# Graph attention kernel: three step buffers, more compares on VectorE, sums and reciprocals on GpSimd

## The chip, the cores and the metric

The kernel runs on one core of a Trainium2 chip. The metric is the device time of one execution in microseconds, lower is better. PE is TensorE's matmul (PEld its weight load), DVE is VectorE, ACT is ScalarE, POOL is GpSimd, and SP is the engine whose queue issues most DMAs.

## The reference

One graph attention layer with a residual and a layer norm. B = 8 batches, N = 2048 nodes, F = 512 features, H = 8 heads of O = 64.

```
h   = x @ W[head]                                  (per batch and head)
s1  = h . a1[head];  s2 = h . a2[head]
e   = leaky_relu(s1[i] + s2[j], slope 0.2)
att = softmax over j of (e where adj[i, j] > 0, else a very negative number)
out = layernorm(x + concat over heads of att @ h)
```

## The kernel before

The softmax is never formed. exp(leaky_relu(s1 + s2)) is a product of a factor of i and a factor of j on either side of the sign of s1 + s2. So the kernel needs only 0/1 masks (adjacency and sign) as stationary operands of matmuls: one set, m_pos, where the sum is positive, and one, m_neg, where it isn't. The denominators are a 65th column of the same matmuls.

A **unit** is one head of one block of 512 nodes i. There are 4 blocks and 32 units in a batch, 256 units in all; k counts blocks, h heads, u all units. Work on the engines for a unit:

- PE `spread_s1` (L449) spreads the head's row of s1 over 128 partitions of a PSUM bank. It is done two units ahead, between the halves of a unit.
- ACT `compare` (L607) makes the step of s1 + s2 for most of the 16 chunks of j (128 nodes each), 512 wide, into m_pos. DVE `compare` (L811) makes the others from s1_bc, a copy that SP loads from DRAM (`load_s1`, L311). `dve_slots` says which chunks are DVE's.
- DVE `make_pos` (L825, twice) ands the step with the transposed adjacency maskT; `make_neg` (L832) makes m_neg from both.
- PE multiplies: the positive half, 64 matmuls of 130 columns (L530) into banks 0 and 1; then the negative half, 128 of 65 columns (L561, L562) into bank 2 or 3.
- DVE `take_pos` (L670) empties banks 0 and 1 (semaphore pos_read, which PE wants before the next positive half). DVE `take_neg` scales the negative half (L677), adds both (L679) and inverts the denominators (L681). POOL `divide_unit` scales these (L991) and multiplies (L996) into y.

m_pos, m_neg, total and s1_bc have two buffers each. A compare for a unit therefore waits until the unit two before it has been multiplied and its m_neg made. DVE's order in the iteration of unit u is: masks of u + 1 with take_pos(u) between m_pos and m_neg, a maximum over a tile of x, statistics or normalisation if any, compare(u + 2), take_neg(u). For the last unit of a batch all the masks of the next batch's unit 0 come before take_pos.

Ahead of the units of a batch stands the **projection**: 16 chunks, for which PE multiplies x by W in float32 (L499, eight matmuls a chunk, three banks in turn) and DVE writes high parts and products (`split_chunk`: L794, L796, L797, L799), POOL the low parts (L1035, L1037). Within it DVE also makes the step and masks of unit 1 (and 0 in the first batch). Its next batch's x tiles are loaded, transposed (L416) and copied (L579) in units 0 to 22 of the batch before; the score matmuls (L427, L435, L456, L462) are in units 24 to 27, and the statistics in units 28 to 30: `score_maxima`, an all-reduce on POOL (`spread_maxima`, L982), `exponents`, `no_edge` and `turn_s2` (L767 last), which the next compare of unit 0 waits for.

The adjacency for the next block comes in eight pieces: SP loads, ACT cuts to 8 bits (L573), SP transposes (L323). In the first block of a batch all eight are cut in unit 0's iteration on ACT, that is during the projection; in the others one or so per unit.

A finished block gets its residual x by an accumulating DMA from POOL (`residual`, L1002) in head 0 of the next block; `ln_first_half`, `ln_statistics` and `ln_apply` (L686, L690, L703) stand in heads 1, 2 and 3, POOL's `deviation` (a pow, L986) in head 3, and the store in SP's queue at head 5.

Of the kernel before, what the change touches and what calls it, by code (L numbers as in the profile page):

```python
# [20 lines left out]
P = 128  # L21
# [22 lines left out]
DVE_SLOTS = {1: {0: (7,), 1: ()}, 2: {0: (7,), 1: (7,)}, 3: {0: (6, 7), 1: (7,)}}  # L44
# [17 lines left out]
def gat_kernel(nc, x, adj, W, a1, a2, out):  # L62
# [39 lines left out]
    with ExitStack() as ctx:  # L102
# [34 lines left out]
        m_pos = [sb(f"m_pos{i}", [P, JC // 2, 2 * BLK], FP8) for i in range(2)]  # L137
# [37 lines left out]
        prod_d = sb("prod_d", [P, 512], F32)  # L175
        x_sum = sb("x_sum", [P, F], F32)

        mean_f = sb("mean_f", [P, H, O1], F32)
        mean_part = sb("mean_part", [P, H, O1], F16)
# [4 lines left out]
        den_inv = [sb(f"den_inv{i}", [P, IT], F32) for i in range(2)]  # L184
# [68 lines left out]
        neg_made = sem("neg_made", free=1)  # L253
# [3 lines left out]
        pos_summed = sem("pos_summed", free=1)  # L257
# [49 lines left out]
        def _(sp):  # L307
# [53 lines left out]
            for q in range(PIECES):  # L361
                if q == 4:
                    store_s1(0)
                    sp.wait_ge(s1_stored, 16 * KB)
                    load_s1(0, 0)
                    load_s1(1, 1)
# [4 lines left out]
            with nc.Fori(0, B, engines=[sp.engine], hint_back_edge=True) as b:  # L371
                for k in range(KB):
                    g = b * KB + k
                    for h in range(H):
# [5 lines left out]
                        if unit == UNITS - 2:  # L380
                            sp.wait_ge(s1_stored, 16 * KB * (b + 2))
                        load_s1(u + 2, h % 2)
# [10 lines left out]
                        for t in range(JC):  # L393
                            if LOAD_UNIT[t] == unit > 0:
                                load_x(JC * (b + 1) + t, t % 2, ((b + 1) * (JC // 2) + t // 2) % (NBLK * IT // 2))
                        if unit == STURN_UNIT + 1:
                            store_s1(b + 1)
                        if h == 5:
# [12 lines left out]
        def _(pe):  # L411
# [35 lines left out]
            def spread_s1(unit):  # L447
# [37 lines left out]
            for unit in range(2):  # L485
                spread_s1(unit)

            with nc.Fori(0, B, engines=[pe.engine], hint_back_edge=True) as b:
                for jc in range(JC):
                    if jc == 0:  # L490
                        pe.wait_ge(s1_T_copied, b + 1)
                    if jc == 1:
# [9 lines left out]
                for k in range(KB):  # L502
                    g = b * KB + k
                    for h in range(H):
# [11 lines left out]
                        for qd in range(QUADS):  # L516
# [5 lines left out]
                            for it in range(IT):  # L522
                                acc = slot(0, it)
                                for j in range(qd * JQ, (qd + 1) * JQ):
# [3 lines left out]
                                    mask = chunk(m_pos[hp], j, it * P, P).bitcast(FP8_WIDE)  # L528
# [8 lines left out]

                        if unit == UNITS - 2:
                            pe.wait_ge(s1_T_copied, b + 2)
                        spread_s1((unit + 2) % UNITS)  # L540
# [16 lines left out]
                        for it in range(IT):  # L557
                            acc = ps[:, 2 + hp, it * O1:(it + 1) * O1]
# [528 lines left out]
```

## Time and profile before

| what | value |
| --- | --- |
| median of 3 runs | 2871.23 us (2862.51 to 2875.33) |
| profiled execution, own time | 2872.58 us |
| its span | 2870.6 us |
| PE / DVE / ACT / POOL busy | 2669.8 / 2510.0 / 2337.4 / 1077.6 us |
| mean granted clock of PE | 0.978 |
| chain that ended last, by engine | ACT 36%, PE 28%, DVE 16%, issue 13%, DMA 3% |

Busy times are unions over a span in which stages differ, so a high share doesn't name the bound; the stages are read one by one further down. The chain follows the last instruction back through what released each step. A wait for several semaphores is shown under the one that came last.

### The profile page before, as it was taken

Reading aid. Unit: us, or ns where it says so; the run is one execution under the profiler, and the core shown is the slowest. Engines: PE = TensorE matmul, PEld = TensorE weight load, DVE = VectorE, ACT = ScalarE, POOL = GpSimd, SP = SyncE. Lnnn points to the kernel's source line nnn. Section 1 sums busy time; section 2 is a strip of 40 time slices with the busy share of each in tenths; the row PEclk is TensorE's granted clock in tenths of the full one; section 3 lists DMA queues with packets and bytes.
Section 4 is the critical chain, followed back from the end, with each engine's and each line's share of the span. In section 5 each row is a group of like instructions: output and inputs, shape, how many; then the busy total and the mean of one; then the engine's idle time right before and its main releaser. Section 6 shows DMA issues by size and latency. Waiting matters only on the chain.

```text
span 2870.6 us, 126143 instructions
## 1 busy us (share of the span) xinstructions
PE 2669.8 (93%) x52546; PEld 2317.7 (81%) x52546; DVE 2510.0 (87%) x3828; ACT 2337.4 (81%) x3894; POOL 1077.6 (38%) x1011
## 2 busy tenths in 40 slices
PE   6999999999999899999999999899998999899996
PEld 3699867988589895898949998499984998759986
DVE  6898978999789988899888998889988999889996
ACT  3699974999669994799938998399983999839995
POOL 4633335333343324433253332633326233263332
PEclk9999999999999999999999999999999999999998
DMA  6467652676527754377543775447744577445773
GB/s 177 119 132 175 150 141 72 142 173 143 142 65 165 175 137 117 72 177 169 136 104 87 176 164 128 118 93 174 165 120 120 111 173 150 124 105 126 175 150 99
DMA packets 281206, 390.20 MB, mean 136 GB/s; under 512 B 161857, under 2 KB 161857, under 8 KB 280673
## 3 DMA queue, kind: packets, MB, share of 16 engines
q1 hardware_dynamic: 253536, 315.24, 41.4%
q0 software_dynamic: 27136, 67.12, 15.0%
q8 instruction: 424, 6.95, 1.0%
q14 instruction: 110, 0.89, 0.1%
HBM read 313.52 MB, written 34.14 MB: 121 GB/s over the span
## 4 chain that ended last, share of the span: by engine, by line
ACT 36%; PE 28%; DVE 16%; issue 13%; DMA 3%; POOL 1%; DVEq 0%; ACTq 0%; SPq 0%; POOLq 0%
ACT m_pos L607 33%; PE ps L530 10%; PE ps L499 5%; PE ps L561 5%; PE ps L562 5%; DMA y<-in_x 3%; DVE m_neg L832 3%; ACT adj_cut L573 2%; DVE m_pos L825 2%; DVE prod L796 2%; ACT xT L579 1%; DVE prod_d L799 1%; DVE m_pos L811 1%; DVE b_both L794 1%; PE ps L435 1%
## 5 line engine op out<-in xcount | busy, mean ns | idle before, releaser
L607 ACT ACTIVATE m_pos<-ps,s_steep 128x512 fp8e4<-128x512 f32 x3440 | 2092.7, 1068 | 354.0 <-PE ps L449 302.8
L530 PE MATMUL ps<-b_both,m_pos 128*128 128x130 f16 x16384 | 1019.4, 221 | 80.3 <-DVE total L670 52.0
L561 PE MATMUL ps<-d_hi,m_neg 128*128 128x65 f16 x16384 | 1039.1, 194 | 20.6 <-issue 20.2
L562 PE MATMUL ps<-d_lo,m_neg 128*128 128x65 f16 x16384 | 1038.7, 194 | 7.1 <-issue 6.7
L562 PEld LDWEIGHTS ps<-d_lo,m_neg 128*128 128x128 fp8e5 x16384 | 1010.3, 98 | 38.8 <-issue 25.4
L530 PEld LDWEIGHTS ps<-b_both,m_pos 128*128 128x128 fp8e5 x16384 | 964.2, 98 | 92.5 <-issue 91.4
L561 PEld LDWEIGHTS ps<-d_hi,m_neg 128*128 128x128 fp8e5 x16384 | 1019.7, 98 | 17.6 <-issue 17.2
L825 DVE TENSOR_TENSOR m_pos<-m_pos,maskT 128x1024 uint32<-128x1024 uint32 x512 | 633.0, 1255 | 156.1 <-ACT m_pos L607 140.0
L991 POOL TENSOR_TENSOR den_scaled<-den_inv,bound 128x4 f32<-128x4 f32 x256 | 251.3, 982 | 1260.5 <-DVE den_inv L681 1204.0
L832 DVE TENSOR_TENSOR m_neg<-m_pos,maskT 128x2048 uint32<-128x2048 uint32 x256 | 583.8, 2280 | 0.3
L499 PE MATMUL ps<-W_sb,xT 128*128 128x512 f32 x1024 | 461.7, 612 | 45.3 <-DVE prod_d L799 43.4
L573 ACT ACTIVATE adj_cut<-adj_in 128x1024 fp8e4<-128x1024 int32 x264 | 367.5, 1456 | 118.1 <-DMA adj_in<-in_adj 118.1
L499 PEld LDWEIGHTS ps<-W_sb,xT 128*128 128x128 f32 x1024 | 199.7, 197 | 301.9 <-issue 241.7
L811 DVE TENSOR_SCALAR m_pos<-s_bc,s_neg 128x512 fp8e5<-128x512 f32 x656 | 282.3, 482 | 10.4 <-DVE s_neg L767 4.3
L996 POOL TENSOR_TENSOR y<-total,den_scaled 128x256 f32<-128x256 f32 x256 | 281.0, 1098 | 22.6 <-POOL den_scaled L991 2.3
L533 PE MATMUL ps<-mean,tiny_bf 128*128 128x65 f16 x1024 | 198.9, 194 | 0.0
L670 DVE TENSOR_REDUCE total<-ps 128x260 f32<-128x520 f32 x256 | 176.7, 690 | 22.4 <-PE ps L530 21.9
L1035 POOL TENSOR_TENSOR b_both<-prod,b_both 128x512 f16<-128x512 f32 x128 | 143.8, 1124 | 101.2 <-DVE prod L796 90.3
L1037 POOL TENSOR_TENSOR d_lo<-prod_d,d_hi 128x512 f16<-128x512 f32 x128 | 177.4, 1386 | 8.9
L579 ACT ACTIVATE xT<-ps 128x512 f32<-128x512 f32 x144 | 149.2, 1038 | 22.9 <-PE ps L416 22.9
L969 POOL DMA_DIRECT2D x_sum<-in_x x128 | 118.3, 924 | 105.0 <-DMA x_sum<-in_x 97.5
L677 DVE TENSOR_TENSOR neg_part<-ps,r_row 128x260 f32<-128x260 f32 x256 | 107.0, 418 | 30.1 <-PE ps L562 29.6
(94 smaller groups left out, 1552.3 us busy)
## 6 DMA issues: line engine op xcount, KB each, us to landing
adj_in<-in_adj SPq DMA_DIRECT2D x266, 512.0 KB, 4.8
s_bc<-s_rows SPq DMA_DIRECT2D x258, 256.0 KB, 3.6
x_in<-in_x SPq DMA_DIRECT2D x134, 256.0 KB, 4.1
x_sum<-in_x POOLq DMA_DIRECT2D x128, 256.0 KB, 4.8
y<-in_x POOLq DMA_DIRECT2D x32, 1024.0 KB, 11.0
out<-y SPq DMA_DIRECT2D x32, 1024.0 KB, 7.4
maskT<-adj_cut SPq DMA_TRANSPOSE x264, 3.9
m_neg<-in_x SPq DMA_DIRECT2D x10, 256.0 KB, 3.7
```

What stands on the lines that cost most here:

```text
L499: mm = pe.matmul(ps[:, H_BANKS[jc % 3], :], xT[:, fc, jc * P:(jc + 1) * P], W_sb[:, fc, :], start=(fc == 0), stop=(fc == FC - 1))
L530: mm = pe.matmul(acc, mask, b_both[:, j, h, :, :], start=(j == 0 and it % 2 == 0), stop=(j == JC - 1 and it % 2 == 1))
L533: pe.matmul(acc[:, 0:O1], tiny_bf[:], mean[:, h, :], start=False, stop=False)
L561: pe.matmul(acc, mask, d_hi[:, j, h, :], start=(j == 0), stop=False)
L562: mm = pe.matmul(acc, mask, d_lo[:, j, h, :], start=False, stop=(j == JC - 1))
L573: nc.scalar.activation(adj_cut8[slot][:], adj_in[slot][:], ACT.Relu, scale=STEEP, saturate=False).then_inc(adj_cut, 1)
L607: ins = nc.scalar.activation(chunk(m_pos[h % 2], j, 0, BLK), ps[:, BANK_S1 + h % 2, :], ACT.Relu, bias=s2_steep[:, j, h:h + 1], scale=STEE ...
L811: ins = V.tensor_scalar(chunk(m_pos[hp], j, 0, BLK).bitcast(FP8_WIDE), s1_bc[hp][:], s2_neg[:, j, h:h + 1], STEP_UP, ALU.is_gt, ALU.mult, ...
L825: V.tensor_tensor(words(m_pos[hp][:, js, :]), words(m_pos[hp][:, js, :]), words(mask[:, js, :]), ALU.bitwise_and).then_inc(pos_made, 1)
L832: V.tensor_tensor(words(m_neg[hp][:]), words(m_pos[hp][:]), words(mask[:]), ALU.bitwise_xor).then_inc(neg_made, 1)
L991: G.tensor_tensor(den_scaled[hp][:], den_inv[hp][:], bound[:].to_broadcast([P, IT]), ALU.mult).then_inc(den_made, 1)
L996: G.tensor_tensor(y[par][:, :, h * O:(h + 1) * O], total[hp][:, :, 0:O], den_scaled[hp][:].unsqueeze(2).to_broadcast([P, IT, O]), ALU.mult ...
```

## The change

- m_pos gets a third buffer, indexed by unit % 3. Compares may run up to two units ahead on ACT; DVE compares unit u + 3 in the iteration of u, and `before(unit)` counts how many units back the buffer's last user is, across the batch's end (32 is no multiple of 3). Unit 2 of each batch is compared during the projection.
- `DVE_SLOTS` and `dve_slots` give DVE 115 chunks a batch by the new rules (82 by the old).
- DVE's order in the iteration of u becomes: make_neg(u + 1), the maximum, take_pos(u), statistics or normalisation, make_pos(u + 2), compare(u + 3), then the scaling of the negative half.
- `take_neg` keeps only the scaling, into one of two buffers neg_part; POOL does the add and inverts with a pow to the power of -1 in `divide_unit`. mean_part now lies in prod_d's memory.
- `spread_s1` runs three units ahead, in the middle of the negative half, and waits for ACT's compare of the unit that used the bank. `load_s1` is three units ahead too.
- The normalisation, deviation and store of a block stand one unit later; `copy_s1` stands in the last unit.

```diff
-DVE_SLOTS = {1: {0: (7,), 1: ()}, 2: {0: (7,), 1: (7,)}, 3: {0: (6, 7), 1: (7,)}}
+DVE_SLOTS = {1: {0: (7,), 1: (7,)}, 2: {0: (6, 7), 1: (7,)}, 3: {0: (6, 7), 1: (6, 7)}}
@@ dve_slots
-        k, h = divmod((unit - 2) % UNITS, H)
-        if unit in (0, 1) or k * H + h == STAT_UNIT:
+        k, h = divmod((unit - 3) % UNITS, H)
+        if unit in (0, 1, 2) or k * H + h == STAT_UNIT:
             return DVE_SLOTS[1]
-        if (k and h in (2, 3)) or k * H + h in (0, STAT_UNIT + 1):
+        if k and h in (3, 4):
             return DVE_SLOTS[2]
         return DVE_SLOTS[3]
+    def before(unit):
+        return {0: UNITS - (UNITS - 2), 1: UNITS + 1 - (UNITS - 1), 2: UNITS + 2 - (UNITS - 3)}.get(unit, 3)
@@ buffers
-        m_pos = [... for i in range(2)]
+        m_pos = [... for i in range(3)]
-        neg_part = sb("neg_part", [P, IT, O1], F32)
+        neg_part = [sb(f"neg_part{i}", [P, IT, O1], F32) for i in range(2)]
@@ SP, the first batch's unit 2, behind the pieces of unit 0
+                        if unit == 0:
+                            with sp.If(b < 1):
+                                load_s1(2, 0)
+                            load_s1(u + 3, (h + 1) % 2)
@@ PE
+            def spread_s1(unit, u):
+                if type(u) is not int:
+                    pe.wait_ge(step_act, at(step_act, QUADS * (u - 1)))
...
+                    if jc == 8:
+                        spread_s1(2, b * UNITS + 2)
...
-                        spread_s1((unit + 2) % UNITS)
...
                         for it in range(IT):
+                            if it == IT // 2 and unit < UNITS - 3:
+                                spread_s1(unit + 3, u + 3)
@@ DVE take_neg
-                V.tensor_tensor(total[hp][:], total[hp][:], neg_part[:], ALU.add).then_inc(total_made, 1)
-                dve.wait_ge(total_made, u + 1)
-                V.reciprocal(den_inv[hp][:], total[hp][:, :, O]).then_inc(den_inverted, 1)
@@ DVE, iteration of a unit
-                        if unit == UNITS - 1:
-                            with dve.If(b < B - 1):
-                                make_masks(u + 1, 0, maskT[0], g + 1)
-                            take_pos(u, h)
...
+                        if unit < UNITS - 1:
+                            make_neg(u + 1, unit + 1)
...
+                        take_pos(u, h)
...
-                        for when, work in ((1, ln_first_half), (2, ln_statistics), (3, ln_apply)):
+                        for when, work in ((2, ln_first_half), (3, ln_statistics), (4, ln_apply)):
...
+                        if unit < UNITS - 2:
+                            for qd in range(QUADS):
+                                make_pos(u + 2, unit + 2, qd, g + 1)
+                        if unit < UNITS - 3:
+                            compare(u + 3, unit + 3, g * (H // 2) + (h + 3) // 2)
@@ POOL divide_unit
+                G.tensor_tensor(total[hp][:], total[hp][:], neg_part[hp][:], ALU.add).then_inc(total_made, 1)
+                pool.wait_ge(total_made, u + 1)
+                G.tensor_tensor(den[hp][:], total[hp][:, :, O], minus_one[:], ALU.pow).then_inc(den_inverted, 1)
                 pool.wait_ge(den_inverted, u + 1)
-                G.tensor_tensor(den_scaled[hp][:], den_inv[hp][:], bound[:].to_broadcast([P, IT]), ALU.mult
+                G.tensor_tensor(den_scaled[hp][:], den[hp][:], bound[:].to_broadcast([P, IT]), ALU.mult
```

## Rows read from the trace of the kernel before

**Rows 1.** The page: busy time, share of the span, instructions, by engine.
```profile
PE 2669.8 (93%) x52546; PEld 2317.7 (81%) x52546; DVE 2510.0 (87%) x3828; ACT 2337.4 (81%) x3894; POOL 1077.6 (38%) x1011
```

**Rows 2.** Windows: stretch, length, busy us of each engine (instructions), granted clock, DMA share.
```profile
1445.12:1508.72 63.60, 57.57 (x129) 25.13 (x129) 53.60 (x90) 22.24 (x33) 40.37 (x35) 0.95 0.44 113
...
1165.50:1232.52 67.02, 67.02 (x1602) 66.08 (x1600) 58.54 (x82) 63.57 (x109) 19.07 (x21) 0.97 0.42 85
...
1232.52:1303.66 71.14, 67.44 (x1612) 65.67 (x1610) 66.74 (x96) 71.14 (x122) 24.16 (x23) 1.00 0.75 175
...
1375.51:1445.12 69.61, 68.76 (x1578) 62.87 (x1576) 60.10 (x100) 61.08 (x105) 18.60 (x20) 1.00 0.51 126
```

**Rows 3.** Timeline of PE: start, length, engine, line, operation, xcount, [idle before it].
```profile
1184.29 0.38 PE L449 MATMUL ps<-s_T,s_pick 96*128 96x512 bf16 x1
...
1192.10 0.38 PE L449 MATMUL ps<-s_T,s_pick 96*128 96x512 bf16 x1
...
1200.39 0.38 PE L449 MATMUL ps<-s_T,s_pick 96*128 96x512 bf16 x1
...
1450.80 4.88 PE L499 MATMUL ps<-W_sb,xT 128*128 128x512 f32 x11
...
1461.71 4.63 PE L499 MATMUL ps<-W_sb,xT 128*128 128x512 f32 x5 [6.03 <-DVE prod_d L799]
...
1513.45 1.00 PE L530 MATMUL ps<-b_both,m_pos 128*128 128x130 f16 x13 [2.23 <-POOL b_both L1035]
```

**Rows 4.** Timeline of ACT, around unit 2's compare in two batches, and one unit.
```profile
1167.08 8.20 ACT L607 ACTIVATE m_pos<-ps,s_steep 128x512 fp8e4<-128x512 f32 x14 [36.74 <-PE ps L449]
...
1217.19 7.62 ACT L607 ACTIVATE m_pos<-ps,s_steep 128x512 fp8e4<-128x512 f32 x13 [0.25 <-PE ps L449]
...
1516.48 8.20 ACT L607 ACTIVATE m_pos<-ps,s_steep 128x512 fp8e4<-128x512 f32 x14 [36.42 <-PE ps L449]
```

**Rows 5.** Timeline of DVE: the end of one unit, and the batch's end.
```profile
1213.34 1.27 DVE L811 TENSOR_SCALAR m_pos<-s_bc,s_neg 128x512 fp8e5<-128x512 f32 x3
...
1214.52 0.42 DVE L677 TENSOR_TENSOR neg_part<-ps,r_row 128x260 f32<-128x260 f32 x1
...
1215.62 2.58 DVE L825 TENSOR_TENSOR m_pos<-m_pos,maskT 128x1024 uint32<-128x1024 uint32 x2
...
1441.25 0.22 DVE L767 TENSOR_SCALAR s_neg<-s_col 128x128 f32<-128x128 f32 x1
...
1458.97 0.90 DVE L794 TENSOR_TENSOR b_both<-ps,k_b 128x512 f16<-128x512 f32 x1
```

**Rows 6.** POOL's L991 and L986 (ns min/median/max), then timelines of POOL and DVE.
```profile
L991 POOL TENSOR_TENSOR den_scaled<-den_inv,bound x256: 191/1209/1269, 122.8 to 2849.6; 128x4 f32<-128x4 f32 x128
...
L986 POOL TENSOR_TENSOR ln_rstd<-ln_var,minus_half x32: 1036/1037/1063, 208.7 to 2863.2; 128x4 f32<-128x4 f32 x32
...
1259.47 1.04 POOL L986 TENSOR_TENSOR ln_rstd<-ln_var,minus_half 128x4 f32<-128x4 f32 x1 [4.93 <-DVE ln_var L698]
...
1259.54 0.89 DVE L811 TENSOR_SCALAR m_pos<-s_bc,s_neg 128x512 fp8e5<-128x512 f32 x2
...
1279.59 0.61 POOL L996 TENSOR_TENSOR y<-total,den_scaled 128x256 f32<-128x256 f32 x1
...
1279.62 1.66 DVE L825 TENSOR_TENSOR m_pos<-m_pos,maskT 128x1024 uint32<-128x1024 uint32 x1 [0.17 <-ACT m_pos L607]
```

**Rows 7.** One wait of the whole span; timelines of DVE, POOL, SP's queue.
```profile
DVE ln_stats L686 <- DMA y<-in_x: 42.2, 13, 10.3
...
1419.88 0.16 DVE L722 TENSOR_REDUCE stat<-xmax 128x1 f32<-128x16 f32 x1
...
1433.98 0.19 POOL L991 TENSOR_TENSOR den_scaled<-den_inv,bound 128x4 f32<-128x4 f32 x1 [6.94 <-issue]
...
97.45 2.28 DVE L832 TENSOR_TENSOR m_neg<-m_pos,maskT 128x2048 uint32<-128x2048 uint32 x1
...
108.17 11.66 SPq L311 DMA_DIRECT2D s_bc<-s_rows  x2
```

More of the change, by code:

```diff
@@ L364, in _ @@
                     sp.wait_ge(s1_stored, 16 * KB)
-                    load_s1(0, 0)
-                    load_s1(1, 1)
+                    for unit in range(2):
+                        load_s1(unit, unit)
                 turn_piece(q, q % 2, 0, q // 2)
@@ L379, in _ @@
                                 store_block(g - 1, 1)
-                        if unit == UNITS - 2:
+                        if unit == UNITS - 3:
                             sp.wait_ge(s1_stored, 16 * KB * (b + 2))
-                        load_s1(u + 2, h % 2)
+                        if unit == UNITS - 1:
+                            sp.sem_inc(waited[sp.engine], 1)
+                            with sp.If(b < B - 1):
+                                load_s1(u + 3, (h + 1) % 2)
+                        elif unit:
+                            load_s1(u + 3, (h + 1) % 2)
                         for t in range(JC):
@@ L527, in _ @@
                                         pe.sem_inc(waited[pe.engine], 1)
-                                    mask = chunk(m_pos[hp], j, it * P, P).bitcast(FP8_WIDE)
+                                    mask = chunk(m_pos[unit % 3], j, it * P, P).bitcast(FP8_WIDE)
                                     mm = pe.matmul(acc, mask, b_both[:, j, h, :, :], start=(j == 0 and it % 2 == 0),
@@ L606, in compare @@
                             j = qd * JQ + c
-                            ins = nc.scalar.activation(chunk(m_pos[h % 2], j, 0, BLK), ps[:, BANK_S1 + h % 2, :], ACT.Relu,
+                            ins = nc.scalar.activation(chunk(m_pos[unit % 3], j, 0, BLK), ps[:, BANK_S1 + unit % 2, :], ACT.Relu,
                                                        bias=s2_steep[:, j, h:h + 1], scale=STEEP, saturate=False)
@@ L799, in split_chunk, with compare @@
                 V.tensor_tensor(full_d, bank, kd, ALU.mult).then_inc(hi_d_made, 1)
-            def compare(u, h, nth, unit):
+            def compare(u, unit, nth):
+                h = unit % H
                 hp = h % 2
-                dve.wait_ge(neg_made, at(neg_made, u - 1))
+                dve.wait_ge(neg_made, at(neg_made, u - before(unit) + 1))
                 dve.sem_inc(waited[dve.engine], 1)
@@ L824, in make_pos, with make_neg @@
                 js = slice(qd * JQ // 2, (qd + 1) * JQ // 2)
[L825 removed]
+                V.tensor_tensor(words(m_pos[unit % 3][:, js, :]), words(m_pos[unit % 3][:, js, :]),
                                 words(mask[:, js, :]), ALU.bitwise_and).then_inc(pos_made, 1)
[L828 to L829 removed]
+            def make_neg(u, unit):
+                mask = maskT[unit // H % 2]
                 dve.wait_ge(unit_done, at(unit_done, u - 1))
                 dve.wait_ge(pos_made, at(pos_made, QUADS * (u + 1)))
[L832 removed]
+                V.tensor_tensor(words(m_neg[unit % 2][:]), words(m_pos[unit % 3][:]), words(mask[:]), ALU.bitwise_xor
                                 ).then_inc(neg_made, 1)
[L835 to L841 removed]
             V.nop().then_inc(x_maxed, start[x_maxed])
```

102 lines of the change are left out of this document (51 added, 51 removed).

## The prediction

> **What bounds the kernel now.** The page first: all of TensorE, VectorE and ScalarE look loaded, 93, 87 and 81% [rows 1], so no average decides and the stages must be read. The windows show one batch's stages: the projection (63.6 us, the 16 chunks of L499) and three of the four blocks of eight units [rows 2]. In block 1 ScalarE is busy 71.14 of 71.14 us: it sets the pace, and block 2 is built alike. In block 0, where it has no adjacency pieces to cut, TensorE is busy all 67.0 us, and block 3 is nearly so (68.8 of 69.6). In the projection ScalarE stands idle 36 us, until the first compare of unit 2 [rows 4], although it is the engine that is short later: m_pos has two buffers, and unit 2's is unit 0's.
>
> TensorE's own need comes from its timeline [rows 3]: from one spread of s1 to the next a unit takes 1192.10 - 1184.29 = 7.81 us, with a transposed tile of x 1200.39 - 1192.10 = 8.29. Blocks: 0: 8 x 7.81 + 6 x 0.48 = 65.4; 1 and 2: 62.5 + 5 x 0.48 = 64.9 each; 3, with no transposes but the score and mean matmuls, about 71 (its window's 68.8 busy, and unit 24 starts some 3 us ahead of it). Sum 266. A batch lasts 1516.48 - 1167.08 = 349.4 us [rows 4], less the projection's 63.6: the unit phase takes 285.8. So 20 us of it are waits, half-clock stretches and unit 0's late start. The projection has its own: TensorE idles 6.03 us after three chunks, for VectorE's prod_d, and the next five matmuls take 4.63 us, where eleven took 4.88 just before the stall [rows 3]: it comes back at 1.2 GHz. Undisturbed, 128 matmuls at the 0.43 us of the eleven are 55 us; 8.7 could go.
>
> **The parts.** *Compares.* By the new slots VectorE has 115 compares a batch, by the old 82 (656 over 8 batches). One costs VectorE 0.40 us (three from 1213.34 to 1214.52 [rows 5]) and saves ScalarE 0.58 (thirteen in 7.62 [rows 4]). Per full block 8 move: ScalarE 71.1 - 4.6 = 66.5, VectorE + 3.2.
>
> *Add and reciprocal.* L677 to the next L825 is 1215.62 - 1214.52 = 1.10 us [rows 5]; 0.42 stays and about 0.03 between instructions: VectorE loses 0.65 a unit, 5.2 a block. Block 1: 66.7 - 5.2 + 3.2, and 0.4 of gaps, is 65.1 us, against TensorE's 64.9. Block 2 is taken the same. All three engines then need 65 to 67 us in blocks 1 and 2: balanced, with little to spare.
>
> *GpSimd.* Each unit gains an add (nearest row: the 128x256 multiply L996, 0.61 us) and a pow (L986, same size and operation, 1.04 us whenever it ran) ahead of the 0.20 and 0.61 that it has [rows 6]: 2.5 us of 8, and its idle time covers that; total has two buffers, so it may end two units later. What can't be read off is what this takes from VectorE. L996 began at 1279.59, just ahead of L825 at 1279.62, and that L825 took 1.66, where two back to back take 2.58 [rows 5]; the other way round L991's median is 1.21 us against a least of 0.19, since it starts with an L825 and waits behind it [rows 6]. So the two exclude each other. The pow seems harmless: it ran 1259.47 to 1260.5 and the two compares that started under it took 0.89, as two always do. Bounds a unit: nothing, and 0.61 + 1.04 + 0.20 + 0.61 = 2.46 if each op blocks for its whole length. The add starts when the 2.28 us m_neg starts and so waits behind it, then runs under the maximum or take_pos, which no row shows blocked; the last multiply now falls on L825 or the compares, where before it mostly met take_pos. I take 0.35 more a unit, one hit of 0.4 in most units, 2.8 a block: VectorE needs 67.9 in blocks 1 and 2.
>
> The Trainium skill ("SBUF — State Buffer", Who interferes with whom) says that a VectorE instruction with two SBUF inputs and a GpSimd one that reads SBUF exclude each other for the whole instruction, whichever issues first going first. The 1.66 agrees; the pow over the compares doesn't show a hold of its whole length. By the rule alone the sum would go to the 2.46.
>
> *Three buffers, order.* ScalarE may compare unit 2 in the projection and be up to two units ahead; it saves a unit's 8 us at the start of each batch. A unit's masks are made one and a half units before TensorE wants them, so a late VectorE stops TensorE only through take_pos, whose bank is wanted again 3.9 us later (the negative half). That cover holds one lag of 3 to 3.5 us. The normalisation puts 5.2 us into three units running, so it is exceeded in blocks 1 and 2, and the 3.0 us by which each of these blocks overruns comes on top: I take 5 us of TensorE's waits a batch. The spread of s1 moves into the negative half at the same 0.22 us, and now waits for ScalarE's compare of two units before, long done.
>
> *Normalisation later.* It waits 42.2 us in 13 places for the residual's DMA [rows 7]; issued about 5 us into a block, and landing some 11 us later (the last block's wait is 10.3), it is in before the third unit reads it, but the last block's 10.3 stays. This is inside the 20 us above, not added. Stores and deviation move with it, no queue behind them is short.
>
> *Batch's end.* The negative half of unit 30, neg(30), starts a unit and a half, 11.8 us, before TensorE's projection at 1445.12. Now s2_neg is made at 1441.25, 8 us into it; ScalarE's compare of the next unit 0 waits for that, unit 0's masks wait for the compare, and take_pos(31) stands behind the masks. VectorE reaches its first chunk 13.85 us after TensorE's, at 1458.97 [rows 5]. In the new order the scores are turned 3 to 6 us into neg(30) and compare(0) ends 11 to 14 us into it: VectorE's first chunk comes 5 to 9 us after TensorE's, and TensorE, three banks ahead, is released at about its 10.3. The stall and its 1.2 GHz stretch go: 8.7 us a batch, in seven batches. Unit 0 waits 2.23 us for the last b_lo [rows 3]; I leave 1.5.
>
> *New waits.* GpSimd's next arithmetic after stat_made (1420.04) is at 1433.98; the all-reduce is between [rows 7]; with an add and a pow queued behind that, take_pos(30) comes 2 to 3 us late: 3 us a batch. In batch 0 alone, load_s1(2) stands in SP's queue behind the pieces of unit 0, at 108 us; VectorE is then at its tenth chunk at 97.5 [rows 7], and waits about 11 with the landing. At the end, add and pow on GpSimd for 0.65 on VectorE: 1.7.
>
> **Sum**, against the profiled execution's 2872.58 (span 2870.6; the median is 2871.23, so the same to 0.1%). Unit phase: 266 + 5 + 3 + 1.5 = 275.5, say 276: 285.8 - 276 = 9.8, times 8, 78. Projection: 7 x 8.7 = 61. Batch 0: -11. Tail: -1.7. 2872.6 - 126 = 2746; I say 2745, 4.4% faster. This case alone: 2700 to 2790 (VectorE's 0.35 between 0.1 and 0.7).
>
> **Rivals.** *TensorE alone sets the pace.* Blocking costs nothing: 266 + 3 a batch, 135 + 61 - 13 = 183 off, 2690. For: VectorE's 65.1 is level with 64.9. Against: the L825 of 1.66.
> *GpSimd's lock eats half.* Each unit loses 0.8 us (the multiply's whole 0.61 and the scaling's 0.20): VectorE needs 65.1 + 6.4 = 71.5 in blocks 1 and 2 and 66 and 71 in the others, unit phase 281 to 283, 2790 to 2810.
> *Slower.* One mechanism: pow and add hold the port to their end and the chain falls on two-input work each time. VectorE's average unit, about 8.0 (65.1 / 8 in block 1, less in block 0), must then grow past the present 285.8 / 32 = 8.93 and the 0.27 a unit that the projection gives back: from 1.2 us a unit. At the full 2.46, less about 0.6 that lies under take_pos and maxima, it is 9.9 a unit, 317 a batch, 8 x 31 - 48 = 200 slower: 3070. For: the 1.66 us; against: the compares under L986 at full speed. The Trainium skill's rule above is on this rival's side.
> *No change.* ScalarE stays the bound in spite of its 8 fewer compares, since it cannot start until the spread in the middle of the negative half; then blocks 1 and 2 stay at 70 and only the projection's gain is left: 2820 to 2860.
>
> **Chances.** My forecast 0.57, TensorE alone 0.12, half eaten 0.15, little or no change 0.08, slower 0.08. Range 2685 to 2835: from the first rival to the start of the last ones. Faster by over 0.5% 0.86, within 0.5% 0.06, slower 0.08; 0.5% is what a measurement of this kernel tells from nothing.
>
> **What would show it.** Right: TensorE's 6 us wait in the projection gone and the stage near 55; ScalarE's 36 us wait cut by a compare of 8; blocks 1 and 2 at 66 to 68 us; some L825 or L811 at 1.5 times their length under GpSimd's multiply; one wait near 11 us at VectorE in batch 0. Wrong: long L825, L832 or L811 under the pow; take_pos waiting for GpSimd's multiply all through; ScalarE busy all of blocks 1 and 2.

## The result, and the profile after

The change makes the kernel 0.6% faster: 2848.94 us (median of 8 runs) against 2864.81 us for the kernel before, run beside it; the ratio is 0.9943, 95% interval 0.9925 to 0.996. The forecast was 2745 us. The profiled execution has a span of 2845.0 us.

The page's busy line and the chain of work that ended last:

```profile
PE 2666.2 (94%) x52546; PEld 2314.2 (81%) x52546; DVE 2501.7 (88%) x3580; ACT 2190.7 (77%) x3630; POOL 1919.3 (67%) x1524
...
PE 53%; DVE 20%; issue 12%; ACT 6%; POOL 4%; DMA 3%; SPq 1%; DVEq 1%; ACTq 0%; POOLq 0%
```

ScalarE lost 147 us of work [rows 1] and fell from 36% of the chain to 6%. The load moved as planned, yet the time hardly did. The windows of one batch: its projection, blocks 0 to 3 and the pause behind it (columns as in [rows 2], engines PE, PEld, DVE, ACT, POOL):

```profile
1099.50:1154.75 55.25, 55.25 (x129) 24.42 (x130) 51.00 (x87) 23.03 (x35) 41.09 (x37) 1.00 0.51 124
1154.75:1226.31 71.56, 68.57 (x1601) 67.08 (x1600) 65.63 (x82) 53.70 (x91) 51.87 (x37) 0.95 0.39 92
1226.31:1294.77 68.46, 65.58 (x1603) 64.19 (x1599) 64.91 (x87) 66.81 (x111) 50.03 (x37) 1.00 0.75 177
1294.77:1365.12 70.35, 66.24 (x1602) 64.48 (x1599) 65.14 (x89) 67.31 (x112) 51.91 (x40) 1.00 0.74 171
1365.12:1441.80 76.68, 73.65 (x1637) 67.59 (x1633) 60.01 (x97) 57.51 (x98) 42.58 (x39) 0.98 0.50 126
1441.80:1444.54 2.74, 0.06 (x3) 0.01 (x1) 1.23 (x1) 2.74 (x5) 0.00 (x0) 1.00 0.02 6
```

The projection is at 55.25 us, where it was 63.60 [rows 2]. In blocks 1 and 2 ScalarE is no longer busy throughout, but neither is another engine: 66.8 and 67.3 us for ScalarE, 65.6 and 66.2 for TensorE, 64.9 and 65.1 for VectorE, in stages of 68.5 and 70.4. Block 3 is longer than before, and the last window is new.

The waits that answer to those of before (engine, line, what it waited for: us in total, times, longest):

```profile
ACT xT L603 <- PE ps L431: 234.2, 20, 27.8
DVE m_pos L850 <- ACT m_pos L632: 118.8, 83, 2.8
PE ps L551 <- DVE total L694: 28.3, 26, 3.1
PE ps L520 <- issue: 20.3, 7, 3.4
PE ps L551 <- issue: 18.2, 18, 2.6
PE ps L585 <- issue: 15.1, 23, 2.5
DVE ln_stats L707 <- DMA y<-in_x: 14.6, 4, 12.3
PE ps L586 <- issue: 7.3, 10, 1.3
```

ScalarE's idle time of 36 us in the projection [rows 4] is still 27 us long, now ahead of the first tile copy: it has done unit 2's compare and has nothing more it may do. The residual's wait fell from 42.2 us [rows 7] to 14.6.

### The profile page after: what moved, and what is told of

Its sections match the earlier page's. It is cut to its first block, busy times and chain, and to the rows that moved or that the text cites. A ratio compares the mean times of both kernels' runs of the same rounds, so it can differ in the third digit from the quotient of the medians.

```text
span 2845.0 us, 127095 instructions
## 1 busy us (share of the span) xinstructions
PE 2666.2 (94%) x52546; PEld 2314.2 (81%) x52546; DVE 2501.7 (88%) x3580; ACT 2190.7 (77%) x3630; POOL 1919.3 (67%) x1524
## 3 DMA queue, kind: packets, MB, share of 16 engines
q8 instruction: 432, 7.08, 1.1%
## 4 chain that ended last, share of the span: by engine, by line
PE 53%; DVE 20%; issue 12%; ACT 6%; POOL 4%; DMA 3%; SPq 1%; DVEq 1%; ACTq 0%; POOLq 0%
PE ps L551 20%; PE ps L585 10%; PE ps L586 10%; PE ps L520 7%; ACT m_pos L632 5%; DVE m_pos L850 4%; DVE m_pos L836 3%; DVE m_neg L857 3%; DMA adj_in<-in_adj 2%; DVE prod L819 1%; DVE total L694 1%; PE ps L450 1%; PE ps L431 1%; DVE prod_d L822 1%; DVE y L724 1%
## 5 line engine op out<-in xcount | busy, mean ns | idle before, releaser
L632 ACT ACTIVATE m_pos<-ps,s_steep 128x512 fp8e4<-128x512 f32 x3176 | 1906.2, 902 | 178.6 <-PE ps L468 90.6
L585 PE MATMUL ps<-d_hi,m_neg 128*128 128x65 f16 x16384 | 1076.3, 194 | 15.1 <-issue 15.1
L586 PE MATMUL ps<-d_lo,m_neg 128*128 128x65 f16 x16384 | 1075.0, 194 | 7.6 <-issue 7.3
L585 PEld LDWEIGHTS ps<-d_hi,m_neg 128*128 128x128 fp8e5 x16384 | 1039.1, 98 | 18.6 <-issue 17.6
L1014 POOL TENSOR_TENSOR total<-total,neg_part 128x260 f32<-128x260 f32 x256 | 600.9, 2347 | 513.9 <-DVE neg_part L702 447.9
L850 DVE TENSOR_TENSOR m_pos<-m_pos,maskT 128x1024 uint32<-128x1024 uint32 x512 | 619.0, 1237 | 120.2 <-ACT m_pos L632 118.8
L597 ACT ACTIVATE adj_cut<-adj_in 128x1024 fp8e4<-128x1024 int32 x264 | 315.5, 1258 | 189.9 <-DMA adj_in<-in_adj 189.8
L836 DVE TENSOR_SCALAR m_pos<-s_bc,s_neg 128x512 fp8e5<-128x512 f32 x920 | 446.2, 544 | 10.9 <-DMA s_bc<-s_rows 6.6
L1016 POOL TENSOR_TENSOR den<-total,minus_one 128x4 f32<-128x4 f32 x256 | 313.5, 1225 | 20.2
L603 ACT ACTIVATE xT<-ps 128x512 f32<-128x512 f32 x144 | 113.9, 791 | 234.3 <-PE ps L431 234.2
L1018 POOL TENSOR_TENSOR den_scaled<-den,bound 128x4 f32<-128x4 f32 x256 | 164.5, 643 | 20.1
```

The costliest lines, as they stand in the source:

```text
L585: pe.matmul(acc, mask, d_hi[:, j, h, :], start=(j == 0), stop=False)
L586: mm = pe.matmul(acc, mask, d_lo[:, j, h, :], start=False, stop=(j == JC - 1))
L597: nc.scalar.activation(adj_cut8[slot][:], adj_in[slot][:], ACT.Relu, scale=STEEP, saturate=False).then_inc(adj_cut, 1)
L632: ins = nc.scalar.activation(chunk(m_pos[unit % 3], j, 0, BLK), ps[:, BANK_S1 + unit % 2, :], ACT.Relu, bias=s2_steep[:, j, h:h + 1], scal ...
L836: ins = V.tensor_scalar(chunk(m_pos[unit % 3], j, 0, BLK).bitcast(FP8_WIDE), s1_bc[hp][:], s2_neg[:, j, h:h + 1], STEP_UP, ALU.is_gt, ALU. ...
L850: V.tensor_tensor(words(m_pos[unit % 3][:, js, :]), words(m_pos[unit % 3][:, js, :]), words(mask[:, js, :]), ALU.bitwise_and).then_inc(pos ...
```

## TensorE's time, taken apart

For each run the start-to-start times of neighbouring matmuls in the trace were compared with the median for the same pair of lines; an excess over 0.15 us counts as a pause, under the releaser that the trace gives it. A pause "by itself" has none ("issue"): no engine and no data transfer that the profile shows was waited for. Seven steps of 0.40 us in the score matmuls (L435 before, L450 after) are the same in every batch of every run; they are work, and aren't counted as pauses. Us per batch, means of the eight; unit phase is from unit 0's first matmul to unit 31's last; VectorE's column is pauses ahead of a positive half; unit 0's holds b_lo, d_lo and slow matmuls.

| run | unit phase | by itself, in a unit | VectorE | by itself, between units | unit 0 | projection, batches 1 to 7 | at the jump |
| --- | --- | --- | --- | --- | --- | --- | --- |
| before | 286.0 | 5.8 | 7.3 | 0.8 | 3.7 | 63.7 | 0.2 |
| after | 285.7 | 5.5 | 5.3 | 1.1 | 5.3 | 56.2 | 2.7 |
| x2_old_slots | 290.7 | 6.0 | 9.3 | 1.7 | 5.0 | 56.4 | 2.6 |
| x3_norm_as_before | 293.1 | 5.0 | 12.2 | 0.3 | 5.6 | 57.3 | 2.9 |
| x5_light_vector | 284.4 | 6.2 | 1.6 | 3.1 | 5.1 | 56.9 | 2.8 |
| x6_small_pieces | 278.3 | 1.7 | 3.1 | 0.8 | 5.1 | 56.5 | 2.7 |
| x8_three_totals | 282.8 | 5.8 | 3.1 | 0.4 | 5.6 | 56.2 | 2.5 |
| x13_all_light | 276.3 | 2.5 | 0 | 1.4 | 5.1 | 57.3 | 2.5 |
| x14_before_small_pieces | 284.5 | 0.7 | 10.5 | 0.8 | 3.8 | 63.1 | 0.2 |

Without the four columns of pauses 268.5 us are left before and after, and 267 to 270 in every row; that still holds the half-speed matmuls outside unit 0, whose excess is too short to count. So the prediction's 266 us of pure work was nearly right. What failed is what it took the pauses to be. Two of them, in block 1 of the changed kernel (timeline of PE, pause in brackets):

```profile
1247.03 0.91 PE L551 MATMUL ps<-b_both,m_pos 128*128 128x130 f16 x13 [1.32 <-issue]
1252.88 0.19 PE L585 MATMUL ps<-d_hi,m_neg 128*128 128x65 f16 x1 [1.10 <-issue]
```

They come at the same few places of the program, batch after batch, most of them multiples of 123 to 126 matmuls apart. That points to the blocks in which TensorE's program is loaded. These have a DMA queue of their own; its page row, with packets, MB and share of 16 engines, is `q8 instruction: 432, 7.08, 1.1%`, so 16 KB a packet, one every 5.3 us. The packets' times in the trace bear this out. Of the 67 pauses by itself in the changed kernel (of its unit matmuls, all eight batches), 55 ended 1.25 to 1.75 us after such a packet had landed; of 38 pauses for another engine, 5 did. Before the change it was 52 of 77, and none of 50. The two pauses above end 1.45 and 1.37 us after their packet. So most of these pauses end when a block of the program has come. Why the block comes late isn't shown by this; x6 and x14 below show that the data traffic has a part in it.

## The experiments

All stand against the kernel before, run beside them.

**x1: the sum back on VectorE.** The add and the reciprocal return to `take_neg`, and the add and the pow go from `divide_unit` (not shown here).

```diff
                 V.tensor_tensor(neg_part[hp][:], neg, r, ALU.mult).then_inc(neg_read, 1)
+                V.tensor_tensor(total[hp][:], total[hp][:], neg_part[hp][:], ALU.add).then_inc(total_made, 1)
+                V.reciprocal(den[hp][:], total[hp][:, :, O]).then_inc(den_inverted, 1)
```

> The changed kernel with the add and the reciprocal back on VectorE, GpSimd as it was. Theory A (TensorE's own pace holds the time, and GpSimd's help is worth having): VectorE gets back 0.65 us a unit and loses the collisions (about 65 us in all), so 100 us more busy, of which some 40 to 60 reach the end: ratio to the kernel before about 1.01. Theory B (what GpSimd takes from VectorE's port, and the late take_pos at a batch's end behind its multiply, ate the gain): those waits go, 5 us a batch at least, ratio 0.98.

2848.29 us, 0.9929 (0.9906 to 0.9953): the same as the whole change, so neither theory was right. What moving the sums saves VectorE is worth nothing here.

**x2: the old number of compares on VectorE.** `DVE_SLOTS` as before.

```diff
-DVE_SLOTS = {1: {0: (7,), 1: (7,)}, 2: {0: (6, 7), 1: (7,)}, 3: {0: (6, 7), 1: (6, 7)}}
+DVE_SLOTS = {1: {0: (7,), 1: ()}, 2: {0: (7,), 1: (7,)}, 3: {0: (6, 7), 1: (7,)}}
```

> The changed kernel with the old table of slots: 83 compares a batch on VectorE instead of 115. Theory A (in blocks 1 and 2 TensorE and ScalarE are level, so ScalarE becomes the bound again): ScalarE needs 71 us in blocks 1 and 2 where they now take 69 and 70, so 2 to 4 us a batch more, ratio 1.00 to 1.005. Theory B (the compares are where GpSimd's multiply hits VectorE, and VectorE is the bound): ratio 0.985.

2878.8 us, 1.0034 (1.0019 to 1.005), 0.9% slower than with the 115 compares. ScalarE is late again, VectorE waits for it 261.5 us at L850 (118.8 after), and passes that on to TensorE (9.3 a batch).

**x3: the normalisation as before**, in heads 1, 2, 3, with deviation and store.

```diff
-for when, work in ((2, ln_first_half), (3, ln_statistics), (4, ln_apply)):
+for when, work in ((1, ln_first_half), (2, ln_statistics), (3, ln_apply)):
```

> The changed kernel with the normalisation, the deviation and the store back at heads 1, 2, 3 and 5. Theory A (VectorE's waits for the residual's DMA were cover that TensorE didn't notice): same as the changed kernel within 5 us, ratio 0.995. Theory B (they were on the path): 27 us of waits come back and more, since GpSimd issues the residual later, ratio 1.005.

2900.87 us, 1.0108 (1.0088 to 1.0127): the shift is worth 1.65%, the largest part of all. The unit phase is 7.4 us a batch longer, and 6.9 of that are TensorE's waits for VectorE. **x12** asks why: x1 and x3 together.

> The changed kernel with two parts undone together: the sum and the reciprocal back on VectorE (alone 0.9929) and the normalisation at its old units (alone 1.0108). Theory 1 (the shift was needed because GpSimd, with two more operations in each unit and the residual behind them, delivers a block's rows later, and VectorE waits for them): with the sums off GpSimd the rows are in time again, so a ratio of 0.993 to 0.998, and the 17 us of unit 18 go back to about 11. Theory 2 (the normalisation's place relative to VectorE's compares and ands, which now stand later in a unit, is what costs): the loss stays, 1.005 to 1.012.

2883.34 us, 1.0076 (1.005 to 1.0103). Most of the loss stays without the sums on GpSimd, so they aren't its cause. VectorE's timeline in x12, block 2, from unit 17:

```profile
1319.85 2.29 DVE L861 TENSOR_TENSOR m_neg<-m_pos,maskT 128x2048 uint32<-128x2048 uint32 x1
1322.06 0.69 DVE L694 TENSOR_REDUCE total<-ps 128x260 f32<-128x520 f32 x1
1330.21 1.29 DVE L711 BATCH_NORM_STATS2 ln_stats<-y 128x6 f32<-128x512 f32 x2 [7.46 <-DMA y<-in_x]
1331.42 2.34 DVE L854 TENSOR_TENSOR m_pos<-m_pos,maskT 128x1024 uint32<-128x1024 uint32 x2
```

In block 2 (means of six batches, counted from the block's first matmul) the residual's rows land at 24.3 us in x12 and 24.8 in x3, and VectorE comes to them at 17.1 and 15.9. In the kernel before it came at 19.4 and they landed at 21.8; with the shift it comes at 25.2 and waits in one batch of the six, 1.2 us. So of x12's longer wait (7.2 us for 2.4) about half is that VectorE comes earlier, and half that the rows land later; GpSimd issues their DMA 12.6 us into the block there and 11.0 in the kernel before, for a reason that wasn't looked into. While VectorE stands there, the masks of unit 19, take_neg(17) and take_pos(18) stand behind it; unit 18 takes TensorE 17.1 us in x12 and 10.8 after. (The slot rule stays moved in both, so the lighter units 3 and 4 no longer meet the normalisation; how much of the loss is that wasn't taken apart.)

**x4: unit 2's row loaded first in batch 0**, ahead of the pieces.

```diff
+                        else:
+                            with sp.If(b < 1):
+                                load_s1(2, 0)
...
                         if unit == 0:
-                            with sp.If(b < 1):
-                                load_s1(2, 0)
                             load_s1(u + 3, (h + 1) % 2)
```

> The changed kernel with batch 0's load of unit 2's row of s1 ahead of the eight pieces in SP's queue. The projection of batch 0 takes 66.6 us now and 59.2 before. Theory A: it goes back to 59, 7 us off, ratio 0.992. Rival: the wait only moves to another place (the adjacency pieces, delayed by the load): nothing, ratio 0.994.

2839.95 us, 0.9894 (0.9874 to 0.9913). Batch 0's projection fell from 66.6 to 60.0 us. The ratio moved by 0.5%, 14 us, twice as much; the rest has no cause shown. The wait that it removes, in the changed kernel (timelines of SP's queue and of DVE):

```profile
99.87 6.64 SPq L317 DMA_DIRECT2D s_bc<-s_rows  x3
...
105.13 0.89 DVE L836 TENSOR_SCALAR m_pos<-s_bc,s_neg 128x512 fp8e5<-128x512 f32 x2 [6.62 <-DMA s_bc<-s_rows]
```

**x5: VectorE's two ands on an eighth of the data**, which leaves out seven eighths of the masking.

```diff
-                js = slice(qd * JQ // 2, (qd + 1) * JQ // 2)
+                js = slice(qd * JQ // 2, qd * JQ // 2 + 1)
```

> The changed kernel with each and of the step and the adjacency on an eighth of its data, so it leaves out seven eighths of the masking with the adjacency; VectorE has 1.9 us less work in each unit and is nowhere the bound. What TensorE then takes is its own floor. Theory A (the floor is what the traces show when its gaps inside a unit, 15 us a batch, are counted as its own): only its 5 us a batch of waits for VectorE and part of unit 0's go, ratio to the kernel before 0.975 to 0.98. Theory B (the prediction's floor: 266 us of units and 55 of projection): ratio 0.93 to 0.94.

2847.14 us, 0.9928 (0.9899 to 0.9957). With VectorE's waits nearly gone (1.6 us a batch for 5.3) TensorE is hardly faster, and the chain says so: `PE 80%; issue 7%; DVE 4%; ...`. Theory A had expected 0.975 to 0.98; the prediction's floor (theory B) missed by more: a TensorE freed of VectorE still takes 284.4 us. Pauses by themselves are 9.3 us of that, 2.7 more than in the changed kernel.

**x6: adjacency loads an eighth as long**, to thin the traffic; it leaves out 117 of 390 MB.

```diff
-                sp.dma_start(adj_in[slot][:], adj_tiles[... slot * JH * P:(slot + 1) * JH * P]
+                sp.dma_start(adj_in[slot][:, 0:n], adj_tiles[... slot * JH * P:slot * JH * P + n]
```

> The changed kernel in which every adjacency piece after the first two loads only an eighth of its columns; seven eighths of that traffic (117 of 390 MB) are left out, every instruction is still there. Theory A (TensorE's gaps inside a unit, at fixed places of its program some 120 matmuls apart, are instruction blocks that arrive late behind the big transfers of blocks 1 and 2): 5 to 8 of the 8.4 us a batch go, ratio 0.975 to 0.98. Rival (they are something of TensorE itself): ratio 0.994, gaps as they were.

2788.24 us, 0.9727 (0.9703 to 0.9751). The waits of x6, then the rows of its queues:

```profile
PE ps L551 <- issue: 12.1, 20, 1.2
...
PE ps L586 <- issue: 1.9, 3, 0.7
...
PE ps L585 <- issue: 0.8, 2, 0.6
```

```profile
q1 hardware_dynamic: 253536, 197.80, 29.2%
...
q8 instruction: 432, 7.08, 1.1%
```

The unit phase fell by 7.4 us a batch: 3.8 of it are TensorE's own pauses in a unit (5.5 to 1.7), 2.2 are waits for VectorE. The rows of the waits say the same: the three of TensorE's unit matmuls sum to 40.6 us after the change and to 14.8 here. So about two thirds of the pauses hang on the traffic.

**x7: 128 empty instructions at the head of TensorE's program.**

```diff
+            for i in range(128):
+                pe.nop()
             pe.nop().then_inc(x_turned, start[x_turned])
```

> The changed kernel with 128 empty instructions at the head of TensorE's program, where it waits for data, so that the loop lies elsewhere in the blocks in which instructions are fetched. Between a batch's last matmul and the next one's first are 2.9 us now and were 0.2 before. Theory A (the loop's first block is fetched only on the jump, or ahead of it, according to where the loop's ends lie): the gap goes, 7 x 2.7 = 19 us, ratio 0.988. Rival (it comes with the new order): no change, ratio 0.994.

2847.28 us, 0.9926 (0.9902 to 0.995), pauses and jump unchanged. The most frequent pauses even kept their places, counted in matmuls from unit 0's first (2053 and 2177, for example), though 128 more instructions stood ahead of the loop: the places go by the loop's start and not by the program's.

**x8: a third total buffer** (in prod_d's memory), so that take_pos waits for the multiply of three units back.

```diff
-                dve.wait_ge(att_made, at(att_made, u - 1))
+                dve.wait_ge(att_made, at(att_made, u + 1 - min(before(unit), 3)))
-                V.tensor_reduce(total[hp][:], slots(0), AX.X, ALU.add).then_inc(pos_read, 1)
+                V.tensor_reduce(total[unit % 3], slots(0), AX.X, ALU.add).then_inc(pos_read, 1)
```

> The changed kernel with three buffers of the sums (the third lies in prod_d's memory), so that take_pos waits for GpSimd's multiply of three units back. At each batch's end take_pos(30) waits about 4 us for GpSimd, which was busy with the all-reduce; TensorE stands 2.7 us and runs the next 4 us at 1.2 GHz. Theory A: this goes, 4 us a batch, 30 in all, ratio 0.984. Rival (unit 0's masks need the new scores and ScalarE's compare anyhow, so the wait moves on to the projection's start): ratio 0.992 to 0.996.

2824.73 us, 0.9845 (0.98 to 0.989). This is the wait that it takes away; the changed kernel's timelines of POOL, DVE and PE at the end of a batch:

```profile
1418.07 2.30 POOL L1003 PARTITION_ALL_REDUCE stat_all<-stat  x1 [6.66 <-issue]
1428.08 0.73 POOL L1014 TENSOR_TENSOR total<-total,neg_part 128x260 f32<-128x260 f32 x1 [7.71 <-issue]
1428.89 1.06 POOL L1016 TENSOR_TENSOR den<-total,minus_one 128x4 f32<-128x4 f32 x1
1430.03 0.20 POOL L1018 TENSOR_TENSOR den_scaled<-den,bound 128x4 f32<-128x4 f32 x1
1430.31 0.61 POOL L1023 TENSOR_TENSOR y<-total,den_scaled 128x256 f32<-128x256 f32 x1
...
1431.06 0.70 DVE L694 TENSOR_REDUCE total<-ps 128x260 f32<-128x520 f32 x1 [4.37 <-POOL y L1023]
...
1432.16 0.22 PE L551 MATMUL ps<-b_both,m_pos 128*128 128x130 f16 x1 [2.56 <-DVE total L694]
...
1432.24 0.62 PE L551 MATMUL ps<-b_both,m_pos 128*128 128x130 f16 x8
...
1433.42 1.05 PE L551 MATMUL ps<-b_both,m_pos 128*128 128x130 f16 x8
```

GpSimd can do nothing between 1418 and 1428, the all-reduce; take_pos(30) waits for what is queued behind it; TensorE stands 2.56 us, runs on at full speed for 0.8 us, and then eight matmuls take 1.05 us instead of 0.62: 1.2 GHz. Two windows behind the stall (the third number from the end is the granted clock):

```profile
1432.16:1432.98 0.82, 0.82 (x16) 0.82 (x17) 0.79 (x3) 0.00 (x0) 0.75 (x1) 1.00 0.00 0
1432.98:1436.39 3.41, 3.41 (x37) 3.41 (x35) 2.75 (x7) 1.34 (x3) 1.31 (x2) 0.50 0.02 5
```

Units 30 and 31 took 10.2 and 8.7 us, and 8.1 and 7.9 in x8.

**x9, x10, x11: the two gains together, and the jump.** Between the last matmul of a batch and the first of the next the changed kernel loses 2.7 us:

```profile
1441.66 0.20 PE L586 MATMUL ps<-d_lo,m_neg 128*128 128x65 f16 x1
1444.54 1.98 PE L520 MATMUL ps<-W_sb,xT 128*128 128x512 f32 x4 [2.68 <-issue]
```

x9 has x8's and x4's edits. x10 also puts the spreads for the next batch's units 0 and 1 back ahead of the negative halves of units 30 and 31. x11 is x9 with 16 empty instructions at the end of the loop.

```diff
@@ x10, ahead of the negative half
+                        if unit >= UNITS - 2:
+                            if unit == UNITS - 2:
+                                pe.wait_ge(s1_T_copied, b + 2)
+                            spread_s1(unit + 2 - UNITS, u + 2)
@@ x11, behind the negative half
+                        if unit == UNITS - 1:
+                            for i in range(16):
+                                pe.nop()
```

> The changed kernel with both of the edits that helped: a third total buffer (0.9845 of the kernel before, alone) and batch 0's step row of unit 2 loaded ahead of the adjacency pieces (0.9894 alone). Theory 1 (the two take away different waits, of which one stands in batch 0's projection and the other at unit 31 of every batch): the gains add up to about 0.9945 - 0.9845 = 1.0% and 0.3 to 0.5%, so a ratio of 0.979 to 0.982, 2807 to 2815 us. Theory 2 (the load's gain is lost again in batch 0's first units, which wait for the block's masks): no better than the third total alone, 0.984 to 0.986.

> As the run before this one in the list (third total, load first), and the two score-row spreads for the next batch's units 0 and 1 stand before the negative half of units 30 and 31, as they do in the kernel before, not in its middle. It tells where the 2.6 to 3.9 us between the last matmul of a batch and the first of the next come from (0.2 us in the kernel before). Theory 1 (the spread and its wait in the middle of the last negative half disturb what TensorE's queue has prefetched of the loop's head): the pause falls to 0.2 us in all 7 jumps, about 19 us, 0.7% off the time. Theory 2 (it comes from the program's length or layout, or from traffic on the instruction queue at that moment): the pause stays at about 3 us and the time within 0.3% of the other run's.

> As the first run of this list (third total, load first), with 16 empty instructions on TensorE at the end of the loop's body, so that the jump stands elsewhere in the program. Theory 1 (the pause of about 3 us at the jump depends on where the jump's instruction stands relative to the blocks in which the program is fetched): the pause changes, to 0.2 us or to some other value, by more than 1 us. Theory 2 (it does not): 2.6 to 4.5 us as in the other variants, the time within 0.2% of the other run's.

x9: 2824.24 us, 0.985 (0.98 to 0.99), its four runs from 2806.4 to 2835.41. The expected sum of both gains (0.979 to 0.982) didn't come: batch 0's projection is 5.8 us shorter than in x8, but TensorE's own pauses in the profiled execution are 2.8 us a batch longer. x10: 2806.93 us, 0.9802 (0.9779 to 0.9824), four runs within 2 us. x11: 2817.89 us, 0.9828 (0.9783 to 0.9874). The pause at the jump is 2.5 to 2.7 us in all three: neither the spreads' place nor the jump's position explains it. The trace says what the pause is. The records of the loop's own branch on TensorE's sequencer (ns, least, median, most; the least is the loop's end, where it isn't taken), before and after:

```profile
L488 PEldq COMPARE_BRANCH  x8: 88/392/460, 394.2 to 2847.8; - x8
L507 PEldq COMPARE_BRANCH  x8: 88/3072/3719, 403.2 to 2821.0; - x8
```

So TensorE isn't waiting for an engine; the branch back takes 3 us. In each of the seven jumps of the changed kernel a packet of the instruction queue starts 0.4 to 1.1 us into the branch, and the branch ends 1.4 to 1.5 us after that packet has landed, as the pauses inside a unit do. In the kernel before that packet isn't there: the last one started 2.5 to 3.0 us ahead of the branch, and the next 2.4 us or more behind its start. So the pause goes with the late fetch of a block of the program; why it is fetched ahead of the branch before the change and not after it stays open.

The intervals of the three overlap, so that x10's edit is itself worth something isn't shown; it is the best version measured, 2.0% faster than the kernel before and 1.4% than the change (0.9802 / 0.9943).

**x13: x10 with the light ands and the small loads. x14: the kernel before with the small loads.**

> The best version so far (third total, unit 2's row first, the two spreads at their old place; 0.9802) with VectorE's ands on an eighth of the data and the adjacency loads an eighth as long (both leave work out, so its output is not the reference's): nearly all that waits for another engine and half of the traffic are gone, so what is left is TensorE's own time. Theory 1 (half of TensorE's pauses inside the units come from its instruction blocks arriving late behind the data traffic, the other half stays whatever the others do): the gains of the small pieces (0.9727 against 0.994) and of the best version add up, about 0.957 to 0.962, a unit phase near 275 us a batch, not the 266 of the prediction. Theory 2 (the prediction's 266 can be reached once no engine and no transfer is in the way): 0.935 to 0.945.

> The kernel before, with the adjacency loads an eighth as long (it leaves 117 MB of loading out, so its output is not the reference's). Theory 1 (in the kernel before ScalarE paces blocks 1 and 2 and TensorE's late instruction blocks lie under ScalarE's time there): the loads gain little, a ratio of 0.99 to 1.0, against the 0.978 that the same edit gives the changed kernel. Theory 2 (TensorE's pauses stand on the path in both kernels, so the work that the change takes from ScalarE was not what paced the units): the same gain as in the changed kernel, 0.975 to 0.982.

x13: 2763.54 us, 0.9649 (0.9633 to 0.9665), a unit phase of 276.3 us. With no wait for VectorE left and 117 of 390 MB of the traffic gone, the 266 isn't reached: own pauses (2.5 and 1.4) and unit 0 (5.1) are left. The expected ratio was 0.957 to 0.962: x8's gain and the small loads' don't add up, since with the small loads only 3.1 us a batch of waits for VectorE were left to remove.

x14: 2853.41 us, 0.9966 (0.9954 to 0.9979), where the same edit is worth 2.2% after the change. Two waits of x14; the kernel before has 140.0 us and 52.0 us in the same groups:

```profile
DVE m_pos L825 <- ACT m_pos L607: 139.5, 113, 3.4
...
PE ps L530 <- DVE total L670: 73.5, 66, 2.8
```

TensorE's own pauses fell by 5.1 us a batch (5.8 to 0.7), but 3.2 of these came back as waits for take_pos: it only reached sooner the point where VectorE held it, which itself waits for ScalarE as long as it did. So before the change TensorE's pauses lay largely under ScalarE's time; after it they stand on the path.

## Why the prediction was wrong

**The step that failed** is "So 20 us of it are waits, half-clock stretches and unit 0's late start". Most of it is there: own pauses 5.8 + 0.8, waits for VectorE 7.3, unit 0 3.7, which is 17.6, and 2.5 us more work than the 266. But the working then let 10 of the 20 go: it priced what would remain as 5 + 3 + 1.5 us, each a wait for another engine, and put TensorE's own pauses at nothing. These are 6.6 us a batch before and 6.6 after. The 5 + 3 for VectorE were even more than the 7.3 that the kernel before had, so the whole forecast gain of 9.8 us a batch came out of terms that the change didn't lower. The changed unit phase is 285.7 for 275.5: 6.6 of own pauses, 2.5 of work, 3.8 more in unit 0, and 2.7 less for VectorE. Against the rounded 276 that is 8 x 9.7 = 78 us of the 104 missed. The pauses could be read from the waits of the kernel before, three rows that were not used, 37.9 us in all:

```profile
PE ps L561 <- issue: 20.2, 22, 1.8
...
PE ps L530 <- issue: 11.0, 21, 1.3
...
PE ps L562 <- issue: 6.7, 10, 1.3
```

The other 26 us: 19 at the jump and 8 in the projections, less 4 in batch 0, all three below; 2 or 3 are left over.

**ScalarE as the bound before: right, and too small a prize.** x14 shows that ScalarE (with VectorE behind it) held TensorE. x5, x6 and x13 show what came next: a TensorE whose need, with its pauses and unit 0, was already about 280. The rival "no change" had the time right (2820 to 2860, chance 0.08), but for another reason: ScalarE doesn't stay the bound.

**Projection: right.** 55.2 to 57.0 us in batches 1 to 7, against 55; on average 63.7 became 56.2. The stall of 6 us for prod_d and the 1.2 GHz stretch behind it went from all seven. But 2.7 us of the 8.7 comes back at the jump, which nothing in the rows of before announced: 7 x 2.7 = 19 us. And in four of the seven (2, 5, 6 and 7) the granted clock is 0.50 for 3.4 us at the projection's start, behind that pause; those four take 56.9 or 57.0 us, the others 55.25.

**Batch 0: right in kind, 7.4 us for 11.** 59.2 became 66.6; the wait itself is 6.62.

**Take_pos(30) behind the all-reduce: right in kind.** Predicted 3 us a batch, 2.56 of wait and the slow matmuls after it; x8 puts both at 1% of the time, 3 us in the unit phase. **Unit 0** was to wait 1.5 and loses 5.3: b_lo still comes 2.0 late, and d_lo is now late too (1.2), and 2.0 go to slow matmuls: the granted clock is 0.50 for 6.8 us there in five of eight batches, where it was 3.4 us before. That d_lo is late because TensorE is no longer held in the projection is likely, but no run tested it.

**Compares: right.** ScalarE 66.81 and 67.31 us in blocks 1 and 2 for 66.5 forecast. VectorE came out at 64.9 and 65.1 for 67.9, 3 us less than forecast.

**GpSimd's add and pow: right in sign, small.** The multiply's collision, timelines of DVE and POOL:

```profile
162.87 1.23 DVE L836 TENSOR_SCALAR m_pos<-s_bc,s_neg 128x512 fp8e5<-128x512 f32 x2
...
163.09 0.73 POOL L1023 TENSOR_TENSOR y<-total,den_scaled 128x256 f32<-128x256 f32 x1
```

```profile
1241.66 1.21 DVE L850 TENSOR_TENSOR m_pos<-m_pos,maskT 128x1024 uint32<-128x1024 uint32 x1
...
1241.22 1.03 POOL L1016 TENSOR_TENSOR den<-total,minus_one 128x4 f32<-128x4 f32 x1
```

Two compares take 1.23 us under the multiply and 0.89 elsewhere; an and that starts under the pow takes its usual 1.21. All such excesses of VectorE together are some 65 us, 0.25 a unit for the 0.35 taken; nearly all of it lies in the compares. The Trainium skill ("SBUF — State Buffer", Who interferes with whom) says that a VectorE instruction with two SBUF inputs and a GpSimd one that reads SBUF exclude each other for the whole instruction. That is about the ands, not about the compares, which read one tensor. For the multiply the trace agrees: the one that begins at 1243.08, under the and of 1243.02, takes 1.64 us, where it takes 0.61 undisturbed.

```profile
1243.02 1.23 DVE L850 TENSOR_TENSOR m_pos<-m_pos,maskT 128x1024 uint32<-128x1024 uint32 x1
...
1243.08 1.64 POOL L1023 TENSOR_TENSOR y<-total,den_scaled 128x256 f32<-128x256 f32 x1
```

The pow of 128x4, 1.03 us long, shows no such hold. The rival on that rule (3070 us) fell. x1 shows that none of it reaches the time.

**The shift of the normalisation: wrong.** It was priced at nothing, "inside the 20 us". It is worth 1.65%, since in the new order VectorE reaches the residual 2 to 3.5 us earlier in the block, the rows land 2.5 to 3 us later, and it stalls ahead of take_pos. Without it the change would have made the kernel slower.

## What to carry to other kernels

Before pricing the removal of a bound, take the next engine's time apart by what ended each pause: pauses that no engine explains don't go with the other engine's work, and while another engine is the bound they cost little (0.3% here), so they come to light only when it is relieved. Read them in the rows of PE, not of PEld: in x14 the own pauses of the matmuls nearly went, while the weight loads' row of the same line rose from 91.4 to 104.1 us, as it also counts waits for other engines. A full queue of waits in front of one engine is worth reading for order too: where a step that waits for a transfer stands in VectorE's program was worth more than 33 compares. And one buffer more, where a rare long operation (here an all-reduce) sits in a queue, bought 1%.

## What the hardware showed unexpectedly

TensorE stops by itself 6.6 us a batch at fixed places of its program; with 117 MB of 390 less traffic that is 2.5. The trace ties most of these stops to its program's blocks: 55 of 67 end 1.25 to 1.75 us after a 16 KB packet of the instruction queue has landed. The branch back to the loop's start took 2.95 to 3.72 us in the changed kernel and 0.36 to 0.46 before, with such a packet inside the long ones alone. No run changed the program's loading by itself, so what makes a block late, and what changed at the branch, isn't shown. After a stall of 2.56 us TensorE ran at full speed for 0.8 us and only then at 1.2 GHz, for 3.4 us.
